# Three sums in memory instead of four, and twelve row buffers instead of eight, in an attention and mixture-of-experts layer

## What is computed

```
def _expert_apply(xf, w1, b1, w2, b2):
    return jnp.maximum(xf @ w1 + b1, 0.0) @ w2 + b2
...
topk_p, topk_i = jax.lax.top_k(probs, TOP_K)
topk_p = topk_p / jnp.sum(topk_p, axis=-1, keepdims=True)
gates = gates.at[jnp.arange(T)[:, None], topk_i].add(topk_p)
...
return (acc + g[:, None] * _expert_apply(flat, w1, b1, w2, b2), None)
...
x = x + jnp.tanh(g_ffn[0]) * _L0_ffn_ref(...)
```

## Time and profile before

| | us |
|---|---|
| median of 3 runs | 424.71 |
| the 3 runs | 424.87, 424.71, 420.99 |
| the profiled execution, its own time | 426.1 |
| its span, first to last instruction | 424.3 |
| mean granted TensorE clock in it | 0.932 of full |

### The profile page before, as it was taken

How to read it: one execution, slowest core, us unless ns; L and a number is a source line. 1 busy time by engine, 2 the same in 40 slices (tenths; PEclk the granted TensorE clock), 3 DMA queues, 4 the chain that set the end, 5 groups by cost and what they waited for, 6 DMA issues and landing times.

```text
span 424.3 us, 8600 instructions
## 1 busy us (share of the span) xinstructions
PE 345.4 (81%) x2574; PEld 264.3 (62%) x2574; DVE 248.1 (58%) x769; ACT 213.4 (50%) x536; POOL 214.8 (51%) x242
## 2 busy tenths in 40 slices
PE   7799999999999875344687989999989989989900
PEld 5477666666666564233455868878778868868700
DVE  7997888788888677645311444444444444434536
ACT  4794999889888720102123544444444444435300
POOL 8555321111101114777771776777676676747720
PEclk9999999999999987667699999999999999989955
DMA  8799999971040321333234587877777787776698
GB/s 227 217 308 311 307 344 321 330 212 48 16 123 2 82 59 42 116 105 120 106 105 144 79 125 114 136 129 126 126 121 123 123 131 125 121 126 110 83 259 273
DMA packets 65552, 64.44 MB, mean 152 GB/s; under 512 B 6338, under 2 KB 63844, under 8 KB 65508
## 3 DMA queue, kind: packets, MB, share of 16 engines
q1 hardware_dynamic: 50788, 46.83, 37.6%
q0 software_dynamic: 13680, 17.05, 25.7%
q10 hardware_dynamic: 1040, 0.01, 0.1%
HBM read 30.06 MB, written 33.81 MB: 151 GB/s over the span
## 4 chain that ended last, share of the span: by engine, by line
POOL 27%; PE 27%; issue 15%; DVE 13%; ACT 11%; DMA 4%; SPq 1%; POOLq 1%; DVEq 0%; ACTq 0%
POOL sum L470 27%; ACT probs L549 5%; PE psum L1186 4%; PE psum L1233 4%; PE psum L1395 4%; PE psum L1374 3%; DVE nmax L821 3%; PE psum L1286 2%; DMA sum<-ob,xs 2%; PE psum L1087 2%; PE psum L1204 2%; ACT Vx L631 1%; DMA w<-sum 1%; ACT QK L506 1%; DMA x_sb<-in_x_dram 1%
## 5 line engine op out<-in xcount | busy, mean ns | idle before, releaser
L470 POOL DMA_INDIRECT sum<-ob,xs x79 | 123.0, 1557 | 58.8 <-DVE ob L1057 57.6
L821 DVE TENSOR_REDUCE nmax<-psum 128x2 f32<-128x512 f32 x128 | 79.3, 683 | 10.4 <-PE psum L1186 9.7
L1477 PE MATMUL psum<-w,hT 88*128 (+1 forms) x316 | 82.3, 383 | 0.0
L549 ACT ACTIVATE probs<-psum 128x512 f32<-128x512 f32 x128 | 69.4, 597 | 12.5 <-PE psum L1204 11.4
L668 ACT ACTIVATE hT<-psum,b1b 88x128 f32<-88x128 f32 x158 | 48.8, 357 | 49.4 <-PE psum L1468 49.4
L1459 PE MATMUL psum<-w,xT 128*128 x316 | 63.5, 324 | 7.5 <-ACT xT L659 3.8
L1057 DVE TENSOR_SCALAR ob<-psum,gate 128x256 f32<-128x256 f32 x79 | 38.2, 484 | 48.3 <-PE psum L1477 48.3
L1477 PEld LDWEIGHTS psum<-w,hT 88*128 88x128 f32 (+1 forms) x316 | 54.3, 192 | 4.8 <-issue 0.3
L1459 PEld LDWEIGHTS psum<-w,xT 128*128 128x128 f32 x316 | 47.7, 191 | 13.8 <-issue 13.5
L462 POOL DMA_INDIRECT rows_by_block<-Vx,slot x48 | 46.4, 966 | 18.5 <-issue 14.3
L1040 DVE COPY hb<-psum 128x176 f32<-128x176 f32 x79 | 26.9, 341 | 49.1 <-PE psum L1459 49.0
(11 more groups left out here) (177 smaller groups left out, 477.9 us busy)
## 6 DMA issues: line engine op xcount, KB each, us to landing
rows_by_block<-blank SPq DMA_DIRECT2D x1, 10744.0 KB, 38.2
xs<-rows_by_block SPq DMA_DIRECT2D x79, 136.0 KB, 2.5
w<-in_L_ffn_rw_dram SPq DMA_DIRECT2D x2, 2816.0 KB, 21.2
w<-in_L_ffn_rw_dram SPq DMA_DIRECT2D x16, 352.0 KB
sum<-blank SPq DMA_DIRECT2D x4, 1152.0 KB, 13.0
w<-sum SPq DMA_DIRECT2D x16, 256.0 KB, 5.9
sum<-ob,xs POOLq DMA_INDIRECT x79, 3.9
x_sb<-in_x_dram SPq DMA_DIRECT2D x4, 256.0 KB, 4.4
```

Source lines behind the costliest of these rows:

```text
L470: pool.indirect_dma_start(yd[i], bass.IndirectOffsetOnAxis(ap=xs[b % ROWS_AHEAD][:, X_ID:X_ID + 1].bitcast(U32), axis=0), ob[i][:, :], Non ...
L549: act.activation(probs[g % 2][:, :, n, :], st_bank(g, n)[:, :].rearrange("p (t q) -> p t q", t=TB), ACT.Exp, scale=SCALE).then_inc(exp_ok, 1)
L821: dve.tensor_reduce(nmax[i % 2][:, :, n], S_BANK[(4 * i + n) % SB][:, :].rearrange("p (t k) -> p t k", t=TB), AX.X, ALU.max, negate=True). ...
L1477: ins = pe.matmul(Y_BANK[b % 2][:, 0:D], hT[b % 2][0:rows, c, :], w2[0:rows, bass.ds(expert[b], 1), c, :].rearrange("p a n -> p (a n)"), s ...
```

## The change

Two numbers and the size of an unused piece of SBUF change:

```
-    SUMS, ROWS_AHEAD = 4, 8
-    SPARE = 1040
+    SUMS, ROWS_AHEAD = 3, 12
+    SPARE = 208
     assert ROWS_AHEAD % SUMS == 0 and HC < P
```

## The result

The changed kernel takes 402.36 us (median of 4 runs, 402.14 to 402.65) against 424.79 us for the kernel before (median of 4 runs, 420.99 to 431.98). The ratio is 0.950, with a 95% interval from 0.944 to 0.956; it leaves out the slow run of before, 431.98 us, and compares means, 402.4 us with 423.5 us. Forecast were 405 us, within 398 to 416. The profiled execution of the changed kernel has a span of 400.4 us, before 424.3 us: 23.9 us less.

The account below looks back on a forecast made before the run. PE's own work sets 1.905 us per block, and late row loads disturb the loop. Span 424.3 - 21.5 (loop) + 2 (three sums) - 1.5 (end) = 403.3 us, plus 1.8 us around it: 405 us, range 398 to 416.

Parts of the forecast that it names:

- a ring of 15.0 us in 15.24 us: Row buffers: scatter landing 3.9, load 2.5 and transposition lead 8.6 us against eight steps of 1.905 us; margin 0.2 us.
- all disturbances of the loop, 21.5 us: Loop of blocks: 170.1 us less 78 undisturbed steps of 1.905 us; twelve row buffers were to remove this excess.
- the 13.5 us of "issue" ahead of line 1459: PE in the loop: idle time in 26 pieces without named releaser, counted as the wake of late row loads.
- the rival that they are PE's own: Line 1459: reading the expert's number costs the issue time, which stays; only 8 us go, 416.6 us; chance 0.08.
- The lower bound, 13.0 us by name: Loop's gain at least: PE's named waits for row loads, 8.8 us weight side and 4.2 us matmul side.
- The upper end, the whole excess: Loop's gain at most: all 21.5 us above the undisturbed steps; the forecast took this, less new disturbance.
- The ring of three sums: VectorE waits for the scatter three blocks earlier; landings up to 4.95 us hidden; cost taken as 2 us, 0 to 4.
- The rival that this ring turns the gain into a loss: Loop: landings of 6.0 us make steps of 2.26 us, 6 us more than before, about 431 us; chance 0.04.
- The end: After the last scatter's start, 19.3 us: four reads fewer save 3.0 us against a later start; 1.5 us less taken.
- The bound of 1.1 to 1.1 + 3.9 us: End's gain: 1.1 us if reads stay bound by DMA engines, at most 3.9 us more if the last scatter lands sooner.
- The clearing DMA that goes: Early on, SP saves 4.1 us of issue, covered by its later wait of 81.5 us; counted as nothing.
- the 403.3 us worked out: Forecast span: 424.3 less 21.5 for the loop, plus 2 for the sums' ring, less 1.5 at the end.

Follow-up runs that it names:

- E2: The kernel before with twelve row buffers instead of eight, still four sums, spare piece of SBUF left out: 406.3 us.
- E3: The kernel before, four sums and eight row buffers, but VectorE copies row numbers to their own tile, so loads no longer wait for a scatter's landing: 405.06 us.
- E7: The changed kernel itself, unaltered, measured again beside a version with another end: 402.86 us.
- E4: The changed kernel with two sums instead of three, still twelve row buffers: 445.55 us (one run).
- E1: The changed kernel with nine row buffers instead of twelve, still three sums: 404.27 us.
- E5: The changed kernel with six row buffers instead of twelve, still three sums: 543.8 us (one run).

## Why the prediction was right

**The loop.** The step that carried the forecast was that eight buffers make a ring of 15.0 us in 15.24 us, and that all disturbances of the loop, 21.5 us, come from it. They did: 21.6 us went. The decision to count the 13.5 us of "issue" ahead of line 1459 as a wake of the late rows, against the rival that they are PE's own, is borne out: in the changed kernel, in E2 and in E3, which have nothing in common but that a row buffer is free in time, they are 1.0, 0.9 and 1.0 us.

The lower bound, 13.0 us by name, was not well formed. It adds the waits of the weight side and of the matmul side, which are the same stalls seen from two sides, as the row beside the one of 253.49 us shows:

```profile
253.48 0.20 PEld L1450 LDWEIGHTS psum<-ident,xs 128*128 128x128 f32 x2 [1.25 <-DMA xs<-rows_by_block]
```

On the matmul side alone, rows were waited for by name for 4.2 us, and two more waits, in the same view as the earlier trace rows, stand ahead of the first product:

```profile
PE psum L1459 <- ACT xT L659: 3.8, 9, 0.6
PE psum L1459 <- issue: 3.3, 10, 0.4
```

Less 0.3 us that lie before 235 us, the three are 11.0 of PE's 12.1 idle us. So the price of the rival, 416.6 us, which took the 13.5 us of the weight side for time of the loop, was no better founded. The upper end, the whole excess, needed neither sum.

**The ring of three sums.** Here the term was mis-sized: I took 2 us for it, and the loop shows nothing above 78 steps of 1.905 us. The waits are there, 3.0 us on POOL in 8 pieces and 2.1 us on VectorE, in E7 2.7 and 8.2 us, but landings kept their median of 3.9 us and their longest was 5.0 us (E7 5.5 us) though the DMA share rose to 0.82 (I had worked out 0.85). What is lost POOL makes up: in E7 a late scatter starts 2.64 us after the one before, at 311.72 us, and the next ones at 313.58, 315.44 and 317.30 us, 1.86 us apart and not 1.905. The rule of the Trainium skill's page "DMA: Bandwidth & Descriptors", section "Latency and other measured facts", that the memory's latency rises to 2 us at high load, did not show in this stretch: the median landing was the same. Landings did lengthen by 0.5 us in the median in E3, at a DMA share of 0.79, and to 5.57 to 7.75 us where eight or more reads of 256 KB ran beside the last scatter. The rival that this ring turns the gain into a loss needed 5.77 us for every landing; E4 shows what the ring does when it is too short.

**The end.** Forecast was 1.5 us less, measured 2.7 us. The bound of 1.1 to 1.1 + 3.9 us held, and the step that was set too low is the last scatter's landing: I stayed near the 7.75 us of before, and with fewer reads beside it it took 6.04 us, 1.7 us less. The other 1.0 us lies behind that landing, near the 1.1 us of the reads. E1, E2, E3 and E7 give 2.3 to 2.6 us between three and four sums.

**The rest.** The clearing DMA that goes left no trace: the loop begins at 235.3 us instead of 234.9 us, within the spread of that beginning. The two sizes that were off, 2 us of the ring and 1.2 us of the end, less the later beginning, make 2.8 of the 2.9 us by which the span of 400.4 us lies under the 403.3 us worked out.

## What to carry to other kernels

A buffer's ring is everything between two uses of it, also the step that holds it last for a small thing; add its rows up and compare with the number of buffers times the undisturbed step. Here 128 row numbers per block held 136 KB until the scatter had landed, and a ring with 0.2 us to spare on paper, and less than none whenever a landing was late, cost 21 us. One buffer more (E1) brought nearly all of it, and a copy of the numbers (E3) all. Whether a scatter needs its row numbers until it has landed, or only while POOL issues it, no run here shows. When the mean step of a loop lies above its undisturbed one, look at the steps one by one before believing the engine that the chain names.

## What the runs showed of the hardware that was not expected

A late row costs more than its wait. In E5's loop PE is idle for 285.0 - 211.1 = 73.9 us, of which 60.5 us are waits for row buffers. But its 900 matmuls are also busy for 211.1 us, where 917 take 146.25 us in the changed kernel: at a mean granted clock of 0.80 instead of 1.00 that is 65 us more, nearly as much as the idle time.

A scatter that accumulates was slowed more by reads beside it than by its own kind. With scatters and row loads alone, at DMA shares of 0.82 and 0.79, the median landing was 3.9 us (changed kernel) and 4.4 us (E3). With eight reads of 256 KB queued beside it the last scatter landed after 5.57 to 6.37 us, with twelve after 6.95 to 7.75 us, and after 3.97 us in E4, where four reads began 1.4 us behind its start.
